# A third tile's rows in early memory, the first tile in halves, and edge scores one row group a step

## The chip, the cores and the metric

The kernel runs on one core of one Trainium2 chip. The metric is the device time of one execution in microseconds (us), as the median of three runs. The core's engines are named as in the profile: PE is TensorE (PEld its weight loads), DVE is VectorE, ACT is ScalarE, POOL is GpSimd, SP is SyncE, which here only issues DMAs. Each engine works through its own list of instructions in order and waits on semaphores.

## What is computed

One graph layer over 1250 nodes of 1024 features, in float32. Cut to what matters (dst also feeds the choice of edges for each window of nodes):

```python
edge_index = jnp.stack([src, dst])            # 41250 edges, sorted by dst
xn = _layernorm(x, axis=-1)
x = x + gnn(xn, edge_index, W, b)             # relu(A_norm @ (xn @ W) + b)
      + linear_attention(xn, Wq, Wk, Wv, Wo)  # phi = elu + 1, 16 heads, S = phi(K)^T V
x = x + ffn(_layernorm(x, axis=-1))           # two gated, two gelu layers, one out
```

The change touches only the first `_layernorm`, the K/V projection that follows it, and the preparation of the edge lists.

## The kernel before

The 1250 rows are 10 tiles of 128 (the last 98). Weights come as slices of 128x512; each is split into a high part (`weight_hi`, a rounding copy, on ACT here) and a low part (`weight_lo`, the difference, on POOL or DVE), and each product is three matmuls (lines 1383 to 1385 for rows in tiles).

The part around the change is a loop of 40 steps that all engines run in step with each other, `s, t = divmod(step, 10)`: weight slab s (256 columns of K beside 256 of V), row tile t. While slab 0 is worked, the ten tiles are also normalised and transposed, a few steps ahead.

- **SP** issues the loads of x: tiles 0 and 1 at once into the two buffers of `xrow`, then the edges, biases and scales, then tile t as soon as `xn_ready` says that tile t-2 is normalised.
- **DVE** in step n: `transposed_lo(n+1)` (L951), an item of edge work if there is one, then, once PE has finished the unit, `kb` (L1109) and `kmin` (L1110), `ln_stats(n+3)` (L921 to L923), `phik` (L1122), `ksum`, `ln_finish(n+3)` (L939 to L944). Edge work: step 1 `edge_keys`, 2 `edge_constants`, 3 `edge_ranges` with the first of three `edge_score`, 4 the other two, 5 `edge_most` (raises `score_ready`), 8 `edge_bounds` (raises `bounds_ready`).
- **ACT** in step n: `transposed_hi(n+1)` (L695), `ln_apply(n+2)` (L688, raises `xn_ready`), the exponential (L742), the copy of V (L746), `ln_root(n+3)` (L674, a square root).
- **PE** in step n: `transpose_tile(n+1)` (L1365, eight matmuls), the unit's 24 matmuls, then `kv_sum(n-1)` (L1398). Step 0's unit has `transpose_tile(1)` in its middle.
- **POOL** loads ten weight slices, makes the identity for the transposes, some low parts, then constants, among them the zeroing of `st_blk` (L625), reloads, and `partition_all_reduce` (L637) once `score_ready` is raised; behind it stand the low parts of slices 8 and 9, the first of slab 1.

Before the loop, tile 2 takes part in neither the first loads nor the first statistics: it needs the buffer of tile 0, and its statistics stand behind `transposed_lo(0)` and three low parts of weights on DVE, its root and `ln_finish(2)` in step 0. `st_blk` ([128, 8, 128] float32, 4 KB a partition, as much as one tile's rows) holds the block matrix of the attention sums, which is filled only after the 40 steps.

Of the kernel before, what the change touches and what calls it, by code (L numbers as in the profile page):

```python
# [31 lines left out]
P = 128  # L32
# [72 lines left out]
def rows(t):  # L105
    return min(P, N - t * P)
# [50 lines left out]
def build(nc, x, src_cols, dst_cols, dst_rows, wslices, wo, bkv, bq, gb, bo, scales, w3s, out):  # L157
    with ExitStack() as ctx:
# [3 lines left out]
        def sem(name):  # L162
            return ctx.enter_context(nc.semaphore(name))
# [107 lines left out]
        x_in = [sem(f"x_in{i}") for i in range(2)]  # L271
# [155 lines left out]

        def xrows(d, t):
            return d[t * P:t * P + rows(t), :]
# [5 lines left out]
        def _(sp):  # L435
            sp.dma_start(xrow[:, 0, :], xrows(x, 0)).then_inc(x_in[0], 16)
            sp.dma_start(xrow[:, 1, :], xrows(x, 1)).then_inc(x_in[1], 16)
# [7 lines left out]
            for t in range(2, NT):  # L445
                sp.wait_ge(xn_ready, t - 1)
                sp.dma_start(xrow[0:rows(t), t % 2, :], xrows(x, t)).then_inc(x_in[t % 2], 16)
# [143 lines left out]
        def _(pool):  # L591
# [33 lines left out]
            nc.gpsimd.memset(st_blk[:], 0.0).then_inc(consts, 1)  # L625
# [8 lines left out]
            for n in range(KD):  # L634
                reload(n)
            pool.wait_ge(score_ready, 1)
# [34 lines left out]
        def _(act):  # L671
# [5 lines left out]
            def ln_apply(i):  # L677

                t = tile_of(i)
                r = rows(t)  # L680
                act.wait_ge(rstd_ready, i + 1)
                if i >= 2:
                    act.wait_ge(tr_done, 2 * (i - 1))
                if i < NT:
                    to, of = xn[0:r, i % 2, :], xrow[0:r, i % 2, :]
                else:
                    to, of = xn2[0:r, i % 2, :], xr[0:r, (i - NT) % XR_BUFS, :]
                nc.scalar.activation(to, of, ACT.Identity, bias=ln[0:r, i % 2, 5:6],  # L688
                                     scale=ln[0:r, i % 2, 4:5]).then_inc(xn_ready, 1)
# [25 lines left out]
            hi(0)  # L715
            hi(1)
            ln_apply(0)
# [3 lines left out]
            ln_root(1)  # L721
            hi(4)
# [4 lines left out]
            for step in range(40):  # L727
# [3 lines left out]
                if step == 0:  # L731
                    ln_root(2)
# [25 lines left out]
            act.wait_ge(consts, 3)  # L758
# [149 lines left out]
        def _(dve):  # L908
# [7 lines left out]
            def ln_stats(i):  # L916
                t = tile_of(i)
                r = rows(t)
                src = xrow[0:r, i % 2, :] if i < NT else xr[0:r, (i - NT) % XR_BUFS, :]
                for g in range(2):  # L920
                    link(dve.bn_stats(stats[0:r, i % 2, 6 * g:6 * g + 6], src[:, 512 * g:512 * g + 512]))  # L921
# [33 lines left out]
            def edge_keys():  # L955

                dve.wait_ge(edges_in, 48)
                dve.wait_ge(consts, 7)
# [15 lines left out]
            def edge_ranges():  # L974
# [5 lines left out]
                edge_score(0)  # L980

            def edge_scores():
                edge_score(1)
                edge_score(2)
# [97 lines left out]
            dve.wait_ge(x_in[0], 16)  # L1082
# [3 lines left out]
            ln_stats(1)  # L1086
            transposed_lo(0)
            weight_lo(dve, LO_FIRST[0])
            ln_finish(1)
            for n in LO_FIRST[1:]:  # L1090
                weight_lo(dve, n)
            dve.wait_ge(x_in[0], 32)
            ln_stats(2)
            edge_parts = {1: edge_keys, 2: edge_constants, 3: edge_ranges, 4: edge_scores, 5: edge_most, 8: edge_bounds}
            dve_more = None
            for step in range(40):
# [5 lines left out]
                if step == 0:  # L1102
                    ln_finish(2)
                if step in edge_parts:
                    edge_parts[step]()
                u = UNIT["kv", s, t]
# [4 lines left out]
                if step < 7:  # L1111
                    dve.wait_ge(x_in[(step + 3) % 2], 16 * ((step + 3) // 2 + 1))
                    ln_stats(step + 3)
# [235 lines left out]
        def _(pe):  # L1349
# [5 lines left out]
            def transpose_tile(i):  # L1355
# [3 lines left out]
                pe.wait_ge(xn_ready, i + 1)  # L1359
                if i >= 1:  # L1360
                    pe.wait_ge(tr_lo, 2 * i)
                for g in range(2):
                    for j in range(4):
# [306 lines left out]
```

## Time and profile before

| what | value |
|---|---|
| median of 3 runs | 1035.27 us (1034.58 to 1037.59) |
| profiled execution | 1034.41 us, span 1032.5 us |
| PE busy | 994.2 us, 96% of the span |
| DVE busy | 555.1 us, 54% |
| ACT busy | 296.0 us, 29% |
| POOL busy | 142.6 us, 14% |
| chain that ended last | PE 83%, DVE 8%, POOL 3%, issue 3%, ACT 2%, DMA 1% |

The span is measured from the first instruction to the last; the execution's own time has about 1.9 us more around it. The shares of the chain are those of the work that ended last, followed back from the end; PE's share of it, not its busy share, says how much of the time PE itself sets.

### The profile page before, as it was taken

What the parts mean: (1) busy time and instruction counts of PE and PEld (TensorE: products, weight loads), DVE (VectorE), ACT (ScalarE), POOL (GpSimd) and SP (SyncE); (2) the same over time, 40 slices, a digit from 0 to 9 for tenths busy, and PEclk for the clock granted to TensorE, in tenths of its full rate; (3) what the DMA queues carried; (4) which work ended last, traced back from release to release, by engine and by line L of the source; (5) the groups of instructions that cost most, each with busy time, mean ns of one, the idle gap of its engine ahead of it and who ended that gap; (6) DMA issues with size and microseconds to landing.
All of it is one profiled execution on the core that took longest, in us unless ns stands there. A gap on an engine that the chain in (4) does not pass through costs nothing.

```text
span 1032.5 us, 13194 instructions
## 1 busy us (share of the span) xinstructions
PE 994.2 (96%) x4932; PEld 839.0 (81%) x4932; DVE 555.1 (54%) x1033; ACT 296.0 (29%) x566; POOL 142.6 (14%) x192
## 2 busy tenths in 40 slices
PE   4999999999998998999999999999999999999998
PEld 3878887887888987977778688758878899999986
DVE  5886768778754785874111356455555413112354
ACT  5783213213115341341212322122212312135300
POOL 7011001001002023041120000000300303055100
PEclk9999999999999998999999999999999999999999
DMA  7313103013002012121130266444521502010053
GB/s 279 108 53 91 29 18 108 17 32 95 15 28 83 25 45 93 45 91 52 41 104 13 80 210 193 160 166 133 189 77 62 164 1 82 1 41 1 16 188 134
DMA packets 43965, 86.74 MB, mean 84 GB/s; under 512 B 16138, under 2 KB 20598, under 8 KB 43880
## 3 DMA queue, kind: packets, MB, share of 16 engines
q1 hardware_dynamic: 35400, 57.20, 16.7%
q0 software_dynamic: 8480, 28.45, 8.6%
q8 instruction: 48, 0.79, 0.3%
q14 instruction: 37, 0.30, 0.1%
HBM read 61.38 MB, written 23.76 MB: 82 GB/s over the span
## 4 chain that ended last, share of the span: by engine, by line
PE 83%; DVE 8%; POOL 3%; issue 3%; ACT 2%; DMA 1%; DVEq 0%; POOLq 0%; ACTq 0%
PE PS L1383 9%; PE PS L1384 9%; PE PS L1385 9%; PE PS L1489 8%; PE PS L1490 8%; PE PS L1491 8%; PE PS L1547 5%; PE PS L1549 4%; PE PS L1566 3%; PE PS L1567 3%; PE PS L1568 3%; PE PS L1422 3%; POOL ring L425 2%; PE PS L1617 2%; PE PS L1619 2%
## 5 line engine op out<-in xcount | busy, mean ns | idle before, releaser
L1383 PE MATMUL PS<-ring,act_t 128*128 128x512 f32 (+1 forms) x480 | 196.2, 409 | 4.6 <-POOL ring L425 3.8
L1385 PE MATMUL PS<-ring,act_t 128*128 128x512 f32 (+1 forms) x480 | 191.8, 400 | 0.0
L1384 PE MATMUL PS<-ring,act_t 128*128 128x512 f32 (+1 forms) x480 | 191.8, 400 | 0.0
L1489 PE MATMUL PS<-act_t,ring 128*128 128x416 f32 (+1 forms) x432 | 161.0, 373 | 7.8 <-POOL ring L425 5.2
L1490 PE MATMUL PS<-act_t,ring 128*128 128x416 f32 (+1 forms) x432 | 153.4, 355 | 0.0
L1491 PE MATMUL PS<-act_t,ring 128*128 128x416 f32 (+1 forms) x432 | 152.9, 354 | 0.0
L1383 PEld LDWEIGHTS PS<-ring,act_t 128*128 128x128 f32 (+1 forms) x480 | 90.7, 189 | 29.1 <-POOL ring L425 6.7
L1385 PEld LDWEIGHTS PS<-ring,act_t 128*128 128x128 f32 (+1 forms) x480 | 90.3, 188 | 22.7
L1384 PEld LDWEIGHTS PS<-ring,act_t 128*128 128x128 f32 (+1 forms) x480 | 90.4, 188 | 21.2 <-issue 0.5
L1489 PEld LDWEIGHTS PS<-act_t,ring 128*128 128x128 f32 x432 | 82.1, 190 | 14.2 <-POOL ring L425 6.8
L1490 PEld LDWEIGHTS PS<-act_t,ring 128*128 128x128 f32 x432 | 82.2, 190 | 4.3 <-issue 3.6
L1491 PEld LDWEIGHTS PS<-act_t,ring 128*128 128x128 f32 x432 | 82.1, 190 | 0.9
L1182 DVE RECIPROCAL rec<-rec 128x416 f32<-128x416 f32 (+1 forms) x24 | 65.9, 2747 | 0.0
L706 ACT ACTIVATE ctile<-PS 128x160 uint16<-128x160 f32 x80 | 23.4, 301 | 143.6 <-PE PS L1422 142.7
L600 POOL DMA_DIRECT2D stage_x<-in_wslices_dram x48 | 26.0, 547 | 211.7 <-DVE ring L425 207.5
L1040 DVE TENSOR_TENSOR oh_dst<-iota,kcur 128x960 bf16<-128x960 int16 x80 | 52.0, 650 | 0.0
L425 POOL TENSOR_TENSOR ring<-stage,ring 128x512 fp32r<-128x512 f32 x27 | 36.3, 1346 | 108.1 <-ACT ring L712 106.5
L1109 DVE TENSOR_TENSOR kb<-PS,kvb 128x256 f32<-128x256 f32 (+1 forms) x40 | 16.9, 424 | 58.0 <-issue 41.7
L1320 DVE SCALAR_TENSOR_TENSOR hb<-PS,scl,sil 128x416 f32<-128x416 f32 (+1 forms) x12 | 7.8, 651 | 73.1 <-PE PS L1491 73.1
L600 POOL DMA_DIRECT2D stage<-in_wslices_dram x48 | 26.5, 553 | 139.0 <-DVE ring L425 131.5
L1039 DVE TENSOR_TENSOR oh_src<-iota,kcur 128x768 bf16<-128x768 int16 x80 | 44.1, 552 | 0.3
L1422 PE MATMUL PS<-oh_dst,oh_src 128*128 128x160 bf16 x480 | 43.2, 233 | 0.0
(186 smaller groups left out, 1658.8 us busy)
## 6 DMA issues: line engine op xcount, KB each, us to landing
stage<-in_wslices_dram POOLq DMA_DIRECT2D x48, 256.0 KB, 3.2
stage_x<-in_wslices_dram POOLq DMA_DIRECT2D x48, 256.0 KB, 3.2
xr<-x_d SPq DMA_DIRECT2D x18, 512.0 KB, 3.4
phin_d<-phiq SPq DMA_DIRECT2D x8, 625.0 KB, 3.2
xrow<-in_x_dram SPq DMA_DIRECT2D x9, 512.0 KB, 3.7
xh<-in_x_dram SPq DMA_DIRECT2D x18, 256.0 KB
x_d<-xh SPq DMA_DIRECT2D x18, 256.0 KB
x_d<-xr SPq DMA_DIRECT2D x9, 512.0 KB, 2.8
```

The source lines that it names most:

```text
L425: eng.tensor_tensor(ring[:, slot(k), 1, :], stage_buf(n), ring[:, slot(k), 0, :].bitcast(F32), ALU.subtract).then_inc(w_ready, 1)
L600: pool.dma_start(stage_buf(n), wslices[n]).then_inc(stage_in[stage_slot(n)], 16)
L1040: dve.tensor_tensor(oh_dst[:, b], count(WCOLS), pairs(kcur[:, dt % 2, j, 1], WCOLS), ALU.is_equal).then_inc(onehot, 1)
L1182: dve.reciprocal(rec[:, i % 2, 0:n], rec[:, i % 2, 0:n]).then_inc(rec_ready, 1)
L1383: pe.matmul(out_ap, node_rows(0, k, t), ring[:, slot(k0 + k), 0, :], start=(k == 0), stop=False)
L1384: pe.matmul(out_ap, node_rows(1, k, t), ring[:, slot(k0 + k), 0, :], start=False, stop=False)
L1385: ins = pe.matmul(out_ap, node_rows(0, k, t), ring[:, slot(k0 + k), 1, :], start=False, stop=(k == KD - 1))
L1422: ins = pe.matmul(PS[:, b, 0:WCOLS], oh_src[:, o, j // 2, :, j % 2], oh_dst[:, o, j // 2, :, j % 2], start=(j == 0), stop=(j == STATIC_CHU ...
L1489: pe.matmul(out_ap, w[0], x_t[:, 0, k, o:o + n], start=(k == 0), stop=False)
L1490: pe.matmul(out_ap, w[0], x_t[:, 1, k, o:o + n], start=False, stop=False)
L1491: ins = pe.matmul(out_ap, w[1], x_t[:, 0, k, o:o + n], start=False, stop=(k == nk - 1))
L1547: pe.matmul(out_ap, lhs, h_rows(half, 0, st), start=(st == 0), stop=False)
```

## The change

Tile 2's rows are loaded into the memory of `st_blk` right behind tiles 0 and 1, ahead of the edge loads on SP. Tile 3 then takes buffer 0 and tile 4 buffer 1, each one tile earlier than before. Tile 2's statistics and root move ahead of the first transposed tile's low part, and its `ln_finish` follows tile 1's. `st_blk` is zeroed by POOL after tile 2 is normalised. Tile 0 is loaded as two halves of 512 columns on two semaphores and normalised in two halves, which now stands ahead of the copy of weight slice 1 on ACT; the first four transposes wait for the first half only. The three `edge_score` stand in steps 4, 5 and 6 and `edge_most` in step 7.

```diff
+        def x_buf(t):
+            return t if t < 3 else (t - 3) % 2
+        def x_uses(t):
+            return 16 * sum(0 < u <= t and x_buf(u) == x_buf(t) for u in range(NT))
+        def x_tile(t):
+            b = x_buf(t)
+            return xrow[0:rows(t), b, :] if b < 2 else st_blk[0:rows(t)].rearrange("p a b -> p (a b)")
...
-            sp.dma_start(xrow[:, 0, :], xrows(x, 0)).then_inc(x_in[0], 16)
-            sp.dma_start(xrow[:, 1, :], xrows(x, 1)).then_inc(x_in[1], 16)
+            for g in range(2):
+                sp.dma_start(xrow[:, 0, 512 * g:512 * g + 512], x[0:P, 512 * g:512 * g + 512]).then_inc(x_first[g], 16)
+            for t in range(1, 3):
+                sp.dma_start(x_tile(t), xrows(x, t)).then_inc(x_in[t], 16)
...
-            for t in range(2, NT):
-                sp.wait_ge(xn_ready, t - 1)
-                sp.dma_start(xrow[0:rows(t), t % 2, :], xrows(x, t)).then_inc(x_in[t % 2], 16)
+            for t in range(3, NT):
+                sp.wait_ge(xn_ready, t - 1 if t > 4 else t - 2)
+                sp.dma_start(x_tile(t), xrows(x, t)).then_inc(x_in[x_buf(t)], 16)
...
-            nc.gpsimd.memset(st_blk[:], 0.0).then_inc(consts, 1)
...
+            pool.wait_ge(xn_ready, 3)
+            nc.gpsimd.memset(st_blk[:], 0.0).then_inc(consts, 1)
             pool.wait_ge(score_ready, 1)
...
+                if i == 0:
+                    nc.scalar.activation(to[:, 0:512], of[:, 0:512], ACT.Identity, bias=ln[0:r, 0, 5:6],
+                                         scale=ln[0:r, 0, 4:5]).then_inc(xn_first, 1)
+                    to, of = to[:, 512:D], of[:, 512:D]
...
             ln_root(0)
             hi(0)
+            ln_apply(0)
             hi(1)
-            ln_apply(0)
             hi(2)
             hi(3)
             transposed_hi(0)
             ln_root(1)
+            ln_root(2)
...
-                if step == 0:
-                    ln_root(2)
...
                 for g in range(2):
+                    if i == 0:
+                        dve.wait_ge(x_first[g], 16)
                     link(dve.bn_stats(stats[0:r, i % 2, 6 * g:6 * g + 6], src[:, 512 * g:512 * g + 512]))
...
             ln_stats(1)
+            dve.wait_ge(x_in[2], 16)
+            ln_stats(2)
             transposed_lo(0)
             weight_lo(dve, LO_FIRST[0])
             ln_finish(1)
+            ln_finish(2)
             for n in LO_FIRST[1:]:
                 weight_lo(dve, n)
-            dve.wait_ge(x_in[0], 32)
-            ln_stats(2)
-            edge_parts = {1: edge_keys, 2: edge_constants, 3: edge_ranges, 4: edge_scores, 5: edge_most, 8: edge_bounds}
+            edge_parts = {1: edge_keys, 2: edge_constants, 3: edge_ranges, 7: edge_most, 8: edge_bounds}
...
-                if step == 0:
-                    ln_finish(2)
                 if step in edge_parts:
                     edge_parts[step]()
+                if 4 <= step < 4 + ROWS_T:
+                    edge_score(step - 4)
...
-                pe.wait_ge(xn_ready, i + 1)
-                if i >= 1:
+                if i:
+                    pe.wait_ge(xn_ready, i + 1)
                     pe.wait_ge(tr_lo, 2 * i)
                 for g in range(2):
+                    if i == 0:
+                        pe.wait_ge(xn_ready if g else xn_first, 1)
```

## Rows read from the trace of the kernel before

**Rows 1.** The waits of TensorE, 0 to 110 us: total, times, longest
```profile
PE PS L1365 <- ACT xn L688: 14.8, 4, 9.6
```

**Rows 2.** Busy time by stretch: PE, PEld, DVE, ACT, POOL, PEclk, DMA share, GB/s
```profile
20.60:23.90 3.30, 0.01 (x1) 0.01 (x1) 3.12 (x10) 1.28 (x2) 3.17 (x6) 0.81 0.84 269
23.90:29.40 5.50, 5.50 (x17) 4.73 (x18) 3.64 (x13) 5.15 (x8) 0.00 (x0) 0.50 0.88 311
```

**Rows 3.** The chain that ended last, 60 to 96 us: start, duration, what
```profile
63.17 1.08 PE PS L1365 x8
...
70.28 0.87 PE PS L1365 x8
...
77.17 0.68 PE PS L1365 x8
...
83.44 0.44 PE PS L1398 x4
...
89.45 0.44 PE PS L1398 x4
```

**Rows 4.** Timeline of the start, 9 to 13 us
```profile
9.23 0.15 DVE L923 TENSOR_SCALAR ln<-mv 128x1 f32<-128x1 f32 x1
...
10.31 0.63 ACT L712 ACTIVATE ring<-stage 128x512 fp32r<-128x512 f32 x1 [0.32 <-DMA stage<-in_wslices_dram]
10.85 0.58 ACT L695 ACTIVATE act_t<-PS 128x512 fp32r<-128x512 f32 x1
11.46 1.45 DVE L951 TENSOR_TENSOR act_t<-PS,act_t 128x512 fp32r<-128x512 f32 x2 [2.08 <-ACT act_t L695]
...
12.21 0.80 PE L1383 MATMUL PS<-ring,act_t 128*128 128x512 f32 x1 [0.65 <-DVE act_t L951]
```

**Rows 5.** Timeline from 18 to 26 us
```profile
18.46 1.41 DVE L921 BATCH_NORM_STATS2 stats<-xrow 128x6 f32<-128x512 f32 x2
...
20.16 0.40 PE L1385 MATMUL PS<-ring,act_t 128*128 128x512 f32 x1
...
22.60 1.24 ACT L688 ACTIVATE xn<-xrow,ln 128x1024 f32<-128x1024 f32 x1 [2.06 <-DVE ln L944]
...
23.89 1.97 PE L1365 MATMUL PS<-ident,xn 128*128 128x128 f32 x8 [3.34 <-ACT xn L688]
```

**Rows 6.** Timeline of DVE, 29 to 58 us
```profile
29.71 0.33 DVE L959 TENSOR_SCALAR e_hi<-e_src 128x336 int32<-128x336 int32 x1
...
30.81 0.51 DVE L963 SCALAR_TENSOR_TENSOR keys<-e_dst,e_hi 128x336 f32<-128x336 int32 x1
...
38.89 0.12 DVE L967 MEMSET key_off<- 128x80 int16 x1
...
40.43 0.42 DVE L1109 TENSOR_TENSOR kb<-PS,kvb 128x256 f32<-128x256 f32 x1
...
46.13 0.19 DVE L976 MEMSET smax<- 128x160 f32 x1
...
47.73 0.28 DVE L990 TENSOR_SCALAR score<-thr,d_rng 108x80 f32<-108x80 f32 x1
...
49.05 0.42 DVE L1109 TENSOR_TENSOR kb<-PS,kvb 128x256 f32<-128x256 f32 x1
...
57.31 0.42 DVE L1109 TENSOR_TENSOR kb<-PS,kvb 128x256 f32<-128x256 f32 x1
```

**Rows 7.** The DMA queues, 5 to 10 us: packets, MB, share of 16 engines
```profile
q0 software_dynamic: 403, 1.34, 68.3%
q1 hardware_dynamic: 441, 0.58, 32.6%
```

**Rows 8.** Timeline of POOL, 60 to 80 us
```profile
63.72 0.87 POOL L637 PARTITION_ALL_REDUCE sall<-smax  x1 [39.95 <-DVE smax L997]
71.43 1.28 POOL L425 TENSOR_TENSOR ring<-stage_x,ring 128x512 fp32r<-128x512 f32 x1 [6.84 <-issue]
...
73.79 1.31 POOL L425 TENSOR_TENSOR ring<-stage_x,ring 128x512 fp32r<-128x512 f32 x1
```

More of the change, by code:

```diff
@@ L270, in build @@
         small_in = sem("small_in")
-        x_in = [sem(f"x_in{i}") for i in range(2)]
+        x_first = [sem(f"x_first{i}") for i in range(2)]
+        x_in = [sem(f"x_in{i}") for i in range(3)]
+        xn_first = sem("xn_first")
         kvb_in = [sem(f"kvb_in{i}") for i in range(2)]
@@ L684, in ln_apply @@
                 if i < NT:
-                    to, of = xn[0:r, i % 2, :], xrow[0:r, i % 2, :]
+                    to, of = xn[0:r, i % 2, :], x_tile(i)
                 else:
                     to, of = xn2[0:r, i % 2, :], xr[0:r, (i - NT) % XR_BUFS, :]
+                if i == 0:
+                    nc.scalar.activation(to[:, 0:512], of[:, 0:512], ACT.Identity, bias=ln[0:r, 0, 5:6],
+                                         scale=ln[0:r, 0, 4:5]).then_inc(xn_first, 1)
+                    to, of = to[:, 512:D], of[:, 512:D]
                 nc.scalar.activation(to, of, ACT.Identity, bias=ln[0:r, i % 2, 5:6],
@@ L757, in _ @@
             nc.scalar.activation(deg[:, 1, :], deg[:, 0, :], ACT.Sqrt).then_inc(root_deg, 1)
-            act.wait_ge(consts, 3)
+            act.wait_ge(consts, 7)
             s_ps = PS[:, 3:5, :].rearrange("p a (b c) -> p (a b) c", c=P)
@@ L918, in ln_stats @@
                 r = rows(t)
-                src = xrow[0:r, i % 2, :] if i < NT else xr[0:r, (i - NT) % XR_BUFS, :]
+                src = x_tile(i) if i < NT else xr[0:r, (i - NT) % XR_BUFS, :]
                 for g in range(2):
+                    if i == 0:
+                        dve.wait_ge(x_first[g], 16)
                     link(dve.bn_stats(stats[0:r, i % 2, 6 * g:6 * g + 6], src[:, 512 * g:512 * g + 512]))
@@ L957, in edge_keys @@
                 dve.wait_ge(edges_in, 48)
-                dve.wait_ge(consts, 7)
+                dve.wait_ge(consts, 6)
                 link(dve.tensor_scalar(e_hi[:], e_src[:], 7, None, ALU.logical_shift_right))
@@ L979, in edge_ranges @@
                 link(dve.tensor_scalar(d_rng[a, 0, :], d_rng[a, 0, :], 1.0 - WIN, None, ALU.add))
[L980 to L984, printed above, removed]
             def edge_score(t):
@@ L1079, in count_tile @@
                 link(dve.tensor_reduce(cmx[:, dt:dt + 1], csum[:, dt % 2, :], AX.X, ALU.max))
-            dve.wait_ge(x_in[0], 16)
             ln_stats(0)
@@ L1111, in _ @@
                 if step < 7:
-                    dve.wait_ge(x_in[(step + 3) % 2], 16 * ((step + 3) // 2 + 1))
+                    dve.wait_ge(x_in[x_buf(step + 3)], x_uses(step + 3))
                     ln_stats(step + 3)
```

## The prediction, made before the changed kernel ran

> **What bounds the kernel now.** I read the page's busy shares first (the table above): PE is busy 96% of the span, so a change can only pay where PE waits or where it is slowed. The view of waits then says where that is: in the first 110 us PE waits 14.8 us for normalised rows, in four waits, the longest 9.6 us, which is the start itself [rows 1]. The windows and the timeline place the next: PE's last matmul of step 0 starts at 20.16 and lasts 0.40, so it is done at 20.56, and the transposes of tile 2 start at 23.89 after 3.34 us of idleness [rows 5]. That leaves 14.8 - 9.6 - 3.3 = 1.9 us in two later waits. The stretch behind the long wait shows a second price: from 23.9 to 29.4 us PE is busy all the time at a granted clock of 0.50, the lower level of 1.2 GHz [rows 2]. Those 5.6 us up to about 29.5 hold what takes half at 2.4 GHz, so 2.8 us are lost to the clock.
>
> Tile 2 is late because of DVE's order: its statistics start at 18.46, its rows are applied at 22.60 [rows 5], while buffer, transposed tile 0 and three low parts stand ahead.
>
> **The pace without waits.** The chain of work gives it: transposes start at 70.28 and again at 77.17, so a step of PE is 6.89 us [rows 3]. The step with tile 9's transposes is 83.88 - 77.17 = 6.71, the step without any 89.89 - 83.88 = 6.01 (each the end of the key sum) [rows 3].
>
> **Part 1: tile 2 early.** Its statistics now come before transposed tile 0, and `ln_finish(2)` behind `ln_finish(1)`. ACT applies tile 2 right after the copies of tile 1, at about 19 us, in 1.24 us [rows 5], done before PE asks at 20.56. The 3.34 us go. PE also doesn't idle, so I take the clock to stay up. From 23.89 to 77.17 the kernel before needs 53.28 us for seven steps [rows 3, 5]; at 6.89 they are 48.23. That is 5.05 us: 2.8 of clock, 1.9 of the two waits, and 0.35 of slow starts around these. Sum so far: -8.4.
>
> **Part 2: edge scores spread.** What stops the 5.05 from coming whole is DVE. From one `kb` to the next, 49.05 to 57.31, is 8.26 us with two scores [rows 6]. One score is 49.05 - 47.73 = 1.32 [rows 6], so a bare cycle is 5.62. The other items are 31.32 - 29.71 = 1.61 (keys), 40.43 - 38.89 = 1.54 (constants), 47.73 - 46.13 = 1.60 (ranges) [rows 6]. In the new order the cycles of steps 1 to 6 are 7.23, 7.16, 7.22 and three of 6.94, in all 42.43 against PE's 41.34: DVE falls 1.1 us behind. Its cover: from `kb` at 57.31 to the transposes that it feeds at 63.17 are 5.86 us [rows 3, 6], and PE asks 6.89 after it starts step 1: 1.03 us of slack at the beginning. So slack and shortfall cancel, and each step's handover is within 0.1 us of due. I charge +0.3, bounds 0 and 1.0 (the whole shortfall). In the old order with tile 2 early it would be worse: step 3 with 8.54 and step 4 with 8.26.
>
> **Part 3: more bytes ahead of the weights.** PE's first real matmul starts at 12.21, released by the low part (11.46), released by the high part (10.85), which stands on ACT behind the copy of weight slice 3 (10.31 to 10.94), which itself waited for its DMA [rows 4]. That load decides the start. From 5 to 10 us the two queues move 403 packets (1.34 MB, weights) and 441 packets (0.58 MB, edges, 1.3 KB each) [rows 7]: turns by packet, not by byte. Tile 2's 128 rows of 4 KB now stand in the place of the first 130 edge packets (0.17 MB), so 0.35 MB more go by at 1.92 MB in 5 us: 0.9 us. Bounds: 0, if the load isn't what is late, and 1.4, if all 0.52 MB go first. I take +0.9.
>
> The Trainium skill ("DMA: Bandwidth & Descriptors", section "Queues, rings and completion order") says that each DMA engine goes round between the queues with work at packet granularity; near-equal packet counts agree, and this rule speaks against the change. By a split of bytes in equal halves instead, the weights would lose nothing and the sum would be 0.9 us lower.
>
> Tile 2 itself should land at about 8.6 us (1.05 MB of tiles 0 and 1 are through at about 5, then 0.52 MB at half of 0.38 MB per us, and some 0.8 to land); DVE is done with tile 1's statistics at 9.38 [rows 4]. 1.76 us of statistics end near 11.1, and the low part isn't due before 11.46. Covered; without the cover it would be at most those 1.76 us.
>
> **Part 4: the first tile in halves.** Worth nothing here. It makes the transposes start some 1.5 us sooner, but what follows them is behind slice 3's copy, as above. Moving the copy of slice 1 behind it costs nothing either: it ends at 9.5 at the latest, and slice 3's copy can't start before 10.31. Two loads of 2 KB rows instead of one: the small packets of [rows 7] move 0.58 MB in a 32.6% share, 1.78 MB per full share, against 1.96 for the large ones, so 10% of 0.26 + 0.26 MB, 0.1 us, inside Part 3's bounds.
>
> **Part 5: the tail of slab 0.** `score_ready` comes two steps later, and POOL has the first low parts of slab 1 behind it. The score's end at 63.51 to slice 8's low part at 71.43 is 7.9 us (0.87 of it the reduction, 6.84 an idle "issue") [rows 8], and slice 9's ends at 75.10, 11.6 behind [rows 8]. New clock: PE starts step 1 at 20.56 + 0.9 = 21.5, step 8 at 21.5 + 48.23 + 0.3 = 70.0, step 9 at 76.7 and slab 1 at 82.7. `edge_most` ends at about 70.2, slice 8 is ready at 79.4, slice 9 at 81.8; due at 82.7 and 83.4. DVE's six low parts follow from 81.8 at 0.76 each, due at 0.70 each from 84.1: covered by 1.3 us or more. DVE gets to `kb` of step 9 at 86.4, 4 us late, and its sums are ready about 88.5, when PE wants them at 88.3 to 88.8. Here the cover is some 0.3 us. I charge +0.3, bounds 0 and 1.5. `edge_bounds` in step 8 needs only the reduction, ready near 71.3. Zeroing `st_blk` (0.96 us) moves to POOL's 40 us wait for the score and is free; SP's waits come no later than before. Nothing behind step 12 changes, and PE sets the pace there, so what is gained stays.
>
> **Sum.** -3.34 - 5.05 + 0.3 + 0.9 + 0.3 = -6.9 us. The profiled execution would go from 1034.41 to 1027.5. It lies 0.86 below the median of the runs shown; on the median it is 1035.27 - 6.9 = 1028.4.
>
> **Rivals.**
> - *Earlier transposes bring the clock up earlier.* PE begins some 1.5 to 1.9 us sooner with transposes. If these count, the first unit has up to 1.9 us less at the lower clock, worth half of it, 0.9, and with Parts 3 and 5 near zero the time is about 1026.5. Against: in step 0 the transposes come before a gap, and PE will idle longer behind them. The Trainium skill ("TensorE: Matmul & The Clock Gate", section "Part 4: PE-mode transpose") says that transposes don't count as busy in the same way; no row here separates it. 0.12.
> - *A new wait takes part of it.* DVE or POOL is late at step 5 to 10: the full shortfall of 1.0, 1.4 for the loads, 1.5 in the tail, -8.4 + 3.9 = -4.5, and if the clock comes up later in the first unit as well, 1 to 1.7 more: 1030.8 to 1032. For it: margins of 0.1 and 0.3. 0.17.
> - *No change that can be measured.* Idle moves rather than goes: a gap of some 3 us opens again between steps 1 and 8 and takes the clock down for 5.5 us, as after 20.56: 3.3 + 2.8 back of 6.9, about 1034.5. 0.07.
> - *Slower: tile 2's load is late.* `ln_stats(2)` stands ahead of transposed tile 0 on DVE, and PE's start is behind that. It decides from the landing time: every us after 9.7 costs one, and from about 17 on all 6.9 are gone; landing at 19, behind all ten weight slices, gives 1037 to 1039. Against: queue order puts it right behind tile 1. 0.04.
> - The forecast, 1027 to 1030.5: 0.60.
>
> **Range and chances.** The range holds the forecast and reaches to the first two rivals: 1026.2 to 1032.0. About 0.3%, 3.1 us, is what a measurement of this kernel can tell from no change. Faster 0.88, the same 0.08, slower 0.04.
>
> **What the profile after would show.** Tile 2's transposes directly behind step 0's last matmul, with no idle time and a granted clock of 1.00 through 20 to 30 us; the first real matmul at about 13.1, behind a copy of slice 3 that starts at about 11.2; steps of 6.9 to 7.0 from 21.5 on; step 8 at about 70; the reduction on POOL near 70 and no wait of PE for weights at 83. If the first matmul starts after 14, or PE waits for `ln_apply` in steps 3 to 7 by over 0.5 us each, Parts 3 or 2 are wrong. If the clock falls anyway, Part 1 is.

## The result, and the profile after

The changed kernel takes 1029.95 us (median of 6 runs, 1029.33 to 1031.73) against 1035.15 us for the kernel before on the same chip. The ratio is 0.9944, with a 95% interval of 0.9923 to 0.9964: 5.2 us less by the medians, 3.7 to 8.0 by the interval. The forecast was 1028.4 with a range of 1026.2 to 1032.0, and "faster". Run a second time beside the experiments, the same code gave 1029.94 against 1033.63, a ratio of 0.9956 (0.9942 to 0.9970), so 3.7 us (3.1 to 6.0). The gain is real. The 6.9 us forecast lie inside the first interval and outside the second.

The waits of PE in the first 110 us (what waits, for whom: total, times, longest) answer to [rows 1]. They were 14.8 us for normalised rows in four waits.

```profile
PE PS L1384 <- ACT xn L706: 9.6, 1, 9.6
PE PS L1402 <- DVE act_t L973: 2.7, 1, 2.7
PE PS L1384 <- ACT xn L709: 0.4, 2, 0.2
PE PS L1417 <- DVE phik L1139: 0.2, 1, 0.2
```

The 3.3 us wait before tile 2 is gone, and of the two in steps 5 and 6 (1.9 us) 0.2 are left in step 5; as little is new in step 8. What is new stands in the second line: 2.7 us between the first transposes and the first real matmul, 0.65 before. The windows (PE, PEld, DVE, ACT, POOL busy, granted clock, DMA share, GB/s) show the same from the other side, and answer to [rows 2]:

```profile
12.20:14.20 2.00, 0.01 (x1) 0.01 (x1) 1.90 (x6) 2.00 (x7) 1.22 (x1) 1.00 1.03 384
...
22.80:29.70 6.90, 6.90 (x37) 5.73 (x36) 6.27 (x17) 5.46 (x9) 2.86 (x5) 1.00 0.78 261
```

Where the clock stood at 0.50 for 5.5 us, it is now 1.00, and PE doesn't pause. The step that held the slow stretch, from tile 2's transposes to tile 3's, took 9.52 us (23.89 to 33.41) and takes 6.95 (22.85 to 29.80): 2.6 us. But from 12.2 to 14.2 PE does nothing, while the DMA engines are full. The timeline of the start answers to [rows 4]:

```profile
8.10 0.63 ACT L733 ACTIVATE ring<-stage 128x512 fp32r<-128x512 f32 x1 [2.29 <-DMA stage<-in_wslices_dram]
...
9.36 1.42 DVE L943 BATCH_NORM_STATS2 stats<-xrow 128x6 f32<-128x512 f32 x2 [2.36 <-DMA xrow<-in_x_dram]
...
11.68 1.42 DVE L943 BATCH_NORM_STATS2 stats<-st_blk 128x6 f32<-128x512 f32 x2 [0.47 <-DMA st_blk<-in_x_dram]
11.90 0.63 ACT L733 ACTIVATE ring<-stage 128x512 fp32r<-128x512 f32 x1 [0.55 <-DMA stage<-in_wslices_dram]
12.44 1.07 ACT L716 ACTIVATE act_t<-PS 128x512 fp32r<-128x512 f32 x2
...
13.45 1.28 DVE L973 TENSOR_TENSOR act_t<-PS,act_t 128x512 fp32r<-128x512 f32 x2
...
14.19 0.79 PE L1402 MATMUL PS<-ring,act_t 128*128 128x512 f32 x1 [2.67 <-DVE act_t L973]
```

The copy of slice 3 starts at 11.90 instead of 10.31, after 0.55 us of waiting for its DMA. Even slice 0's (8.10) waited 2.29 us for its DMA. Tile 1's rows are in only at 9.36 and tile 2's at 11.68, so tile 2's statistics, which stand ahead on DVE, hold transposed tile 0's low part until 13.45, although its high part was there at 13.0. Real work starts at 14.19: 1.98 us later. The first unit, from there to its last matmul (22.61), then takes 8.42 us, where the kernel before took 7.95 (12.21 to 20.16); experiments 4 and 8 return to this.

Steps 0 to 3, from the same timeline and DVE's own, answer to [rows 5, 6]:

```profile
20.80 1.25 ACT L709 ACTIVATE xn<-st_blk,ln 128x1024 f32<-128x1024 f32 x1
...
22.61 0.40 PE L1404 MATMUL PS<-ring,act_t 128*128 128x512 f32 x1
...
22.85 1.03 PE L1384 MATMUL PS<-ident,xn 128*128 128x128 f32 x8
```

```profile
23.05 0.42 DVE L1126 TENSOR_TENSOR kb<-PS,kvb 128x256 f32<-128x256 f32 x1 [1.29 <-PE PS L1404]
23.51 0.77 DVE L1127 TENSOR_SCALAR kmin<-kb 128x256 f32<-128x256 f32 x1
...
30.65 0.42 DVE L1126 TENSOR_TENSOR kb<-PS,kvb 128x256 f32<-128x256 f32 x1
...
37.86 0.42 DVE L1126 TENSOR_TENSOR kb<-PS,kvb 128x256 f32<-128x256 f32 x1
...
45.16 0.42 DVE L1126 TENSOR_TENSOR kb<-PS,kvb 128x256 f32<-128x256 f32 x1
...
52.10 0.43 DVE L1126 TENSOR_TENSOR kb<-PS,kvb 128x256 f32<-128x256 f32 x1
```

Tile 2 is normalised at 22.05, before PE asks for it, and its transposes follow the last matmul without a gap. The cycles from `kb` to `kb` are 7.60, 7.21, 7.30 and 6.94 us. The kernel's next transposes and sums on PE (61 to 96 us) answer to [rows 3]:

```profile
72.23 0.89 PE L1384 MATMUL PS<-ident,xn 98*128 98x98 f32 x8 [0.15 <-ACT xn L709]
...
78.55 0.61 PE L1417 MATMUL PS<-phik,vt 128*128 128x128 f32 x4
...
84.55 0.61 PE L1417 MATMUL PS<-phik,vt 128*128 128x128 f32 x4
...
90.96 0.71 PE L1417 MATMUL PS<-phik,vt 98*128 98x128 f32 x4 [0.23 <-DVE phik L1139]
91.51 0.62 PE L1426 MATMUL PS<-ksum,kvb 128*128 128x128 f32 x4
```

and the tail on POOL and on DVE to [rows 8]:

```profile
72.78 0.87 POOL L654 PARTITION_ALL_REDUCE sall<-smax  x1 [47.12 <-DVE smax L1014]
80.89 1.28 POOL L427 TENSOR_TENSOR ring<-stage_x,ring 128x512 fp32r<-128x512 f32 x1 [7.24 <-ACT ring L733]
```

```profile
84.66 3.08 DVE L427 TENSOR_TENSOR ring<-stage,ring 128x512 fp32r<-128x512 f32 x4 [3.78 <-POOL ring L427]
```

Slab 0's last sums (L1426, L1407 before) start at 91.51 instead of 95.75. So 4.24 us are gained by then, and the span is 4.0 us shorter, 1028.5 for 1032.5. What the change touches ends there.

**How to compare these runs.** From those sums to the end of the span, 936.8 us are left before and 937.0 after. In the fourteen profiles of this study that remainder lies between 935.2 and 941.8, with no relation to what the edit was: the second profile of the changed kernel has 940.2. In that profile, and in the one with 941.8, the granted clock is 0.98 from 600 to 700 us, where it is 1.00 in the first profile of the changed kernel and in the kernel before. One total therefore can't settle a term of 1 us. The experiments are read by places on PE instead: the first real matmul, the start of tile 2's transposes (T2), and from there the start of tile 9's (T9) and of slab 0's last sums (S).

| kernel | first matmul | unit | T2 | T2 to T9 | T9 to S | S | MB from 2 to 5 us |
|---|---|---|---|---|---|---|---|
| before | 12.21 | 7.95 | 23.89 | 53.11 | 18.75 | 95.75 | 1.00 |
| changed | 14.19 | 8.42 | 22.85 | 49.38 | 19.28 | 91.51 | 0.74 |
| changed, again | 12.59 | 7.75 | 20.58 | 49.16 | 19.15 | 88.89 | 1.02 |
| halves undone | 12.02 | 8.37 | 20.62 | 49.14 | 19.36 | 89.12 | 0.96 |
| only the load undone | 12.08 | 9.10 | 21.42 | 48.59 | 19.33 | 89.34 | 0.94 |
| loads of 64 rows | 14.51 | 8.02 | 22.77 | 49.04 | 18.79 | 90.60 | 0.72 |
| scores as they were | 13.42 | 8.47 | 22.13 | 51.55 | 18.74 | 92.42 | 0.77 |
| tile 2 early alone | 12.68 | 8.39 | 21.31 | 51.93 | 18.73 | 91.97 | 0.98 |
| scores spread alone | 12.08 | 9.08 | 23.85 | 49.85 | 18.81 | 92.51 | 0.99 |
| halves alone | 12.19 | 7.96 | 23.72 | 53.24 | 18.73 | 95.69 | 0.94 |
| low parts first | 12.89 | 8.86 | 21.98 | 49.80 | 18.78 | 90.56 | 0.94 |
| weights held back | 15.94 | 8.57 | 24.74 | 49.32 | 19.32 | 93.38 | 0.92 |
| edge work early | 12.13 | 8.01 | 20.37 | 48.41 | 18.74 | 87.52 | 0.96 |
| start reordered too | 11.23 | 9.87 | 21.82 | 48.27 | 18.74 | 88.83 | 1.02 |

All starts are raw ones of the timeline. "Unit" is the time from the first real matmul to the last of step 0's 24. The last column adds the two queues of the DMA view. Each row is one profile, and the second profile of the changed kernel reaches S 2.62 us before the first, so a difference of a microsecond between two rows isn't by itself the work of the edit. The unit alone differs by 1.35 us (7.75 to 9.10) between kernels in which PE waits for nothing inside it.

### The profile page after: what moved, and what is told of

It reads as the page before. It is cut to its first block, busy times and chain, and to the rows that moved or that the text cites. A ratio compares the mean times of both kernels' runs of the same rounds, so it can differ in the third digit from the quotient of the medians.

```text
span 1028.5 us, 13197 instructions
## 1 busy us (share of the span) xinstructions
PE 992.2 (96%) x4932; PEld 837.0 (81%) x4932; DVE 555.2 (54%) x1033; ACT 296.0 (29%) x567; POOL 142.7 (14%) x192
## 4 chain that ended last, share of the span: by engine, by line
PE 80%; DVE 10%; POOL 3%; issue 3%; ACT 2%; DMA 2%; SPq 0%; DVEq 0%; POOLq 0%; ACTq 0%
PE PS L1508 8%; PE PS L1509 8%; PE PS L1510 8%; PE PS L1402 8%; PE PS L1403 8%; PE PS L1404 8%; PE PS L1566 5%; PE PS L1568 4%; PE PS L1585 3%; PE PS L1586 3%; PE PS L1587 3%; PE PS L1441 3%; POOL ring L427 3%; PE PS L1636 2%; PE PS L1638 2%
## 5 line engine op out<-in xcount | busy, mean ns | idle before, releaser
L1404 PEld LDWEIGHTS PS<-ring,act_t 128*128 128x128 f32 (+1 forms) x480 | 90.2, 188 | 22.8
L1508 PEld LDWEIGHTS PS<-act_t,ring 128*128 128x128 f32 x432 | 82.0, 190 | 14.2 <-POOL ring L427 6.7
L427 POOL TENSOR_TENSOR ring<-stage,ring 128x512 fp32r<-128x512 f32 x27 | 36.4, 1347 | 109.3 <-ACT ring L733 107.8
```

The costliest lines, as they stand in the source:

```text
L427: eng.tensor_tensor(ring[:, slot(k), 1, :], stage_buf(n), ring[:, slot(k), 0, :].bitcast(F32), ALU.subtract).then_inc(w_ready, 1)
L1404: ins = pe.matmul(out_ap, node_rows(0, k, t), ring[:, slot(k0 + k), 1, :], start=False, stop=(k == KD - 1))
L1508: pe.matmul(out_ap, w[0], x_t[:, 0, k, o:o + n], start=(k == 0), stop=False)
```

## The experiments

My theory after the result: the three parts work as forecast, and the missing 1.7 us or more are at the start (the loads), in DVE's first cycle and in the tail of slab 0. The rivals: the late start is from tile 2's bytes alone; the steps have slack; the tail stands on something else. Each expectation is as it stood before its run.

**1. Halves undone.** The changed kernel with tile 0 whole:

```diff
-            for g in range(2):
-                sp.dma_start(xrow[:, 0, 512 * g:512 * g + 512], x[0:P, 512 * g:512 * g + 512]).then_inc(x_first[g], 16)
-            for t in range(1, 3):
+            for t in range(3):
                 sp.dma_start(x_tile(t), xrows(x, t)).then_inc(x_in[t], 16)
...
-                if i == 0:
-                    nc.scalar.activation(to[:, 0:512], of[:, 0:512], ACT.Identity, bias=ln[0:r, 0, 5:6],
-                                         scale=ln[0:r, 0, 4:5]).then_inc(xn_first, 1)
-                    to, of = to[:, 512:D], of[:, 512:D]
```

> The changed kernel with tile 0 loaded by one DMA and normalised by one operation; everything else as changed. Question: why the first real matmul starts at 14.19 us instead of 12.21. Theory A (tile 2's bytes stand ahead of the weights; the halves cost nothing): first real matmul at 13.8 to 14.3, copy of slice 3 at 11.7 to 12.0, time within 0.5 us of the changed kernel (1030). Theory B (the two half loads slow the first 5 us, in which 0.74 MB arrived instead of 1.00): first real matmul at 12.9 to 13.3, copy of slice 3 at about 11.2, time about 1029.

Measured: 1027.57 us against 1033.80, ratio 0.9936 (0.9916 to 0.9955). The first real matmul comes at 12.02. That is even earlier than theory B had it, and theory A falls: with tile 2's 0.52 MB ahead of the weights the start isn't late at all. The copy of slice 3 ends at 10.75 (copies of slices 1 to 3: 9.00, 1.75 us for three, with no wait for a DMA).

**2. Only the load undone.** One DMA for tile 0, still normalised in halves.

> The changed kernel with tile 0 loaded by one DMA but still normalised in two halves. Theory (only the load costs): first real matmul at 12.0 to 12.5, as with tile 0 whole in both (12.02); the halved normalising itself is worth at most 0.3 us, since slice 3's copy on ScalarE stands ahead of the transposed tile. Rival (the second, longer operation, 2 x 0.80 for 1.24 us, is the cost): 12.4 to 13.

Measured: 1027.63 us against 1033.78, ratio 0.9946 (0.9926 to 0.9966), first matmul at 12.08. Whether the normalising is halved makes no difference to the start (12.02 and 12.08); the load is what does. T2 is 0.8 us later than in experiment 1 all the same, since the unit takes 9.10 us for 8.37. The DMA view from 2 to 5 us (packets, MB, share of the 16 engines), first of this kernel and then of the changed one:

```profile
q1 hardware_dynamic: 246, 0.94, 84.5%
q0 software_dynamic: 1, 0.00, 0.4%
```

```profile
q1 hardware_dynamic: 292, 0.58, 56.1%
q0 software_dynamic: 47, 0.16, 41.7%
```

These are the two kernels' rows in that order. With one load, SP's queue has the engines nearly to itself and brings 0.94 MB. With two short loads, the weights' queue comes in early, with 47 packets instead of 1, and these 47 take 41.7% of 48 engine-microseconds, 0.43 us each, where a packet of theirs takes 0.14 us in [rows 7] (68.3% of 80 for 403). SP's own packets bring 0.58 MB. The second profile of the same kernel is milder: 75 packets of the weights' queue at 0.15 us each, 0.77 MB on SP's, 1.02 together, as much as in the kernel before.

**3. Rows or DMAs?** Tile 0's two loads cut by rows, so that they have 4 KB rows as before:

```diff
-                sp.dma_start(xrow[:, 0, 512 * g:512 * g + 512], x[0:P, 512 * g:512 * g + 512]).then_inc(x_first[g], 16)
+                sp.dma_start(xrow[64 * g:64 * g + 64, 0, :], x[64 * g:64 * g + 64, :]).then_inc(x_first[g], 16)
```

> The changed kernel with tile 0's two loads cut the other way: 64 rows of 4 KB each instead of 128 rows of 2 KB; the same bytes, the same number of DMAs, half the rows to describe. The statistics wait for both. Theory (SP's queue brings about 90 to 100 rows per us, however long they are): about 0.95 MB from 2 to 5 us, first real matmul at 12.0 to 12.7. Rival (one more DMA is what costs): 0.55 to 0.6 MB and first matmul at 13.4 to 14.2 as in the changed kernel.

Measured: 1029.38 us against 1033.78, ratio 0.9955 (0.9939 to 0.9972), first matmul at 14.51. The theory of rows falls:

```profile
q1 hardware_dynamic: 127, 0.45, 61.9%
q0 software_dynamic: 81, 0.27, 37.7%
```

The rows are 4 KB and there are fewer of them, and SP's queue is slower still. The start is lost at another place here: the statistics wait for both loads, and tile 0's begin at 6.85 instead of 4.34. Two short first loads cost, however they are cut; whether by their length or because there is one more of them, these runs don't separate.

**4. Halves alone.** The kernel before with tile 0 in halves and nothing else.

> The kernel before with tile 0 in halves alone (two loads of 2 KB rows, two operations of normalising, slice 1's copy behind them). Theory (the two half loads slow the first 5 us, whatever else is early): 0.55 to 0.60 MB on SP's queue from 2 to 5 us instead of 0.94 to 0.98, first real matmul 13.0 to 13.8 instead of 12.2, time 0.8 to 1.6 us over the kernel before. Rival (only together with tile 2's load): first matmul 12.2, time unchanged.

Measured: 1032.59 us against 1033.78, ratio 0.9991 (0.9979 to 1.0004): no difference. The rival holds: the first matmul is at 12.19. SP's queue is slowed here too (0.71 MB for 0.98), but there is 0.5 MB less to bring before the weights, and slice 3's copy stays at 10.29. PE's timeline of this run bears on the rival of the clock:

```profile
7.74 1.97 PE L1375 MATMUL PS<-ident,xn 128*128 128x128 f32 x8 [7.74 <-POOL ident L608]
12.19 0.80 PE L1393 MATMUL PS<-ring,act_t 128*128 128x512 f32 x1 [2.48 <-DVE act_t L960]
...
15.35 0.61 PE L1394 MATMUL PS<-ring,act_t 128*128 128x512 f32 x1
15.77 0.42 PE L1395 MATMUL PS<-ring,act_t 128*128 128x512 f32 x1
16.03 0.39 PE L1393 MATMUL PS<-ring,act_t 128*128 128x512 f32 x1
```

The transposes begin at 7.74 instead of 9.62, the real matmuls at 12.19 instead of 12.21, and the matmuls change from 0.43 us apart to 0.23 at 15.8 to 16.0, where the kernel before did it too. Matmuls 0.43 us apart are what the kernel before has at a granted clock of 0.50 (26.08 to 29.07), so I read them as the 1.2 GHz level. The windows view doesn't show that level at the start; in the changed kernel it has

```profile
14.10:19.00 4.90, 4.81 (x12) 3.80 (x13) 3.68 (x14) 3.28 (x6) 2.00 (x2) 1.00 1.04 319
```

over matmuls that are 0.43 us apart up to 18.6. In this profile the earlier transposes brought no earlier clock. One pair of profiles doesn't settle it, as experiment 8 shows.

**5. Weights held back.** To see whether the two queues hinder each other, POOL waits with its first weight load until tile 0 is in:

```diff
+            pool.wait_ge(x_first[1], 16)
             for n in range(STAGE_A):
                 load(n)
```

> The changed kernel with GpSimd's first weight loads held back until both halves of tile 0 have landed (about 3.7 us instead of 1.2). Theory (the short first loads cost because the weight packets of the other queue start among them and both then move slowly): SP's queue brings 0.9 MB or more from 2 to 5 us as with one load, tile 2 lands by 8.6, and the first real matmul comes at 12.3 to 13.2 although the weights were asked for 2.4 us later. Rival (it is SP's own queue that is slow behind short loads): still 0.6 MB, first real matmul at 14.5 or later.

Measured: 1032.48 us against 1033.63, ratio 0.9985 (0.9969 to 1.0001); first matmul at 15.94. Half of the theory holds: alone, SP's queue brings 0.92 MB in spite of the halves. The time expected doesn't: POOL issues the first weight load at 4.26 instead of 1.24, the first weight copy starts at 11.04 instead of 8.10, and those 3 us cost more than they save.

```profile
q1 hardware_dynamic: 376, 0.92, 96.2%
```

**6. Scores as they were.** The changed kernel with one score in step 3, two in step 4, `edge_most` in step 5.

```diff
-            edge_parts = {1: edge_keys, 2: edge_constants, 3: edge_ranges, 7: edge_most, 8: edge_bounds}
+            edge_parts = {1: edge_keys, 2: edge_constants, 3: edge_ranges, 5: edge_most, 8: edge_bounds}
...
-                if 4 <= step < 4 + ROWS_T:
-                    edge_score(step - 4)
+                for k in {3: (0,), 4: (1, 2)}.get(step, ()):
+                    edge_score(k)
```

> The changed kernel with the edge scores where they were (step 3 one, step 4 two, edge_most in step 5). Theory of the prediction (DVE sets the pace between steps 1 and 8, 5.62 us plus the item of edge work): steps 3 and 4 have cycles of about 8.6 and 8.3 us on DVE, PE waits for normalised rows some 1.4 + 1.4 us in two places, and the transposes of tile 9 start about 1.5 us later than 72.23; time 1031 to 1032. Against it slab 1's first weights come 9 us sooner on GpSimd, which gives back up to 0.5 us in the tail. Rival (DVE's order has slack, the scores are hidden anyway): tile 9's transposes at 72.2, time as the changed kernel or 0.5 us less.

Measured: 1029.46 us against 1033.80, ratio 0.9953 (0.9940 to 0.9966), so not the expected 1031 to 1032, and by the totals no slower than the changed kernel. PE waits where it was expected to:

```profile
51.59 1.08 PE L1384 MATMUL PS<-ident,xn 128*128 128x128 f32 x8 [1.47 <-ACT xn L709]
...
59.85 1.09 PE L1384 MATMUL PS<-ident,xn 128*128 128x128 f32 x8 [1.16 <-ACT xn L709]
```

DVE's cycles are 8.63 and 8.25 us, and T2 to T9 is 51.55 instead of 49.38: 2.17 us. The tail gives 0.54 back (18.74 for 19.28), so between T2 and S the spreading is worth 1.6 us net. The rival, slack on DVE, is out. The totals don't show the 1.6: this profile starts 0.8 us earlier than the first of the changed kernel (13.42 for 14.19) and reaches S 0.9 us later.

**7. Tile 2 early alone, and 8. scores spread alone.** Each on the kernel before.

> The kernel before with tile 2 early alone (no halves, edge scores where they were, slice 1's copy ahead of tile 0's rows). Theory: nearly all of the gain is here. First real matmul at 13.1 by theory B (14.2 by theory A), no idle time before tile 2's transposes, DVE cycles of 8.6 and 8.3 in steps 3 and 4; time 1030.5 to 1032, so 3.5 to 4.5 us under the kernel before. Rival (the early tile only moves the wait): PE idle 2 us or more before tile 3's or 4's transposes and time above 1033.

> The kernel before with the edge scores spread over steps 4, 5 and 6 alone. Theory: it takes the two waits of PE (0.66 and 1.17 us) in steps 5 and 6, about 1.5 to 2 us together with what stands around them, and slab 1's weights come later with 0.0 to 0.5 us lost in the tail; first real matmul stays at 12.2, the idle time of 3.3 us at 20.6 stays; time 1033 to 1034. Rival (those waits come from being late after tile 2, not from the scores): time unchanged.

Measured: tile 2 alone 1030.19 us against 1033.80, ratio 0.9967 (0.9951 to 0.9982), S at 91.97, 3.78 us earlier; the clock stays up behind step 0 and PE waits 2.6 us in steps 5 and 6, where the kernel before waited 1.8:

```profile
51.11 1.08 PE L1375 MATMUL PS<-ident,xn 128*128 128x128 f32 x8 [1.52 <-ACT xn L703]
...
59.35 1.08 PE L1375 MATMUL PS<-ident,xn 128*128 128x128 f32 x8 [1.09 <-ACT xn L703]
```

Scores alone 1030.69 us, ratio 0.9969 (0.9956 to 0.9982), S at 92.51, 3.24 us earlier. That is more than the expected 1.5 to 2. T2 to T9 falls by 3.26 us, of which 2.2 are the waits and slow starts; the other microsecond is the clock, which came back at about 28.4 here and at 29.5 before, after an idle time of 2.3 us instead of 3.3. That idle time is shorter because step 0 ended later, and that isn't the edit's doing: this kernel's code differs from the one before only from step 3 on, yet its first unit takes 9.08 us for 7.95, with matmuls still 0.43 us apart up to tile 1's transposes:

```profile
16.94 0.63 PE L1382 MATMUL PS<-ring,act_t 128*128 128x512 f32 x1
17.36 1.41 PE L1362 MATMUL PS<-ident,xn 128*128 128x128 f32 x8
```

In the kernel before they were 0.23 us apart from 15.8 on. The unit is 1.13 us longer, which at half speed is some 2.3 us more at the low level. That comes from one execution to the next, and the extra microsecond is luck. The two gains add to 7.0; experiment 1, which has both changes and one load, has 6.6 at S (89.12 for 95.75). An overlap of more than 0.4 us isn't shown.

**9. Low parts first.** POOL makes the low parts of slices 8 and 9 before it waits for the scores:

```diff
             nc.gpsimd.memset(st_blk[:], 0.0).then_inc(consts, 1)
+            for n in range(8, 10):
+                weights(n)
             pool.wait_ge(score_ready, 1)
...
-            for n in range(8, 42):
+            for n in range(10, 42):
```

> The changed kernel with the low parts of slices 8 and 9 on GpSimd ahead of its wait for the scores. Theory (the tail loses 0.5 us because DVE stands 3.8 us behind those low parts): from tile 9's transposes to the end of slab 0's sums 18.75 instead of 19.28 us, no wait of PE for the sums, DVE's low parts from about 81 instead of 84.7; time 0.5 us less than the changed kernel. Rival: DVE's 3.8 us stood on nothing that PE needs, and the 0.5 us are from elsewhere: 19.28 stays.

Measured: 1028.01 us against 1033.78, ratio 0.9939 (0.9921 to 0.9957). T9 to S is 18.78, and DVE reaches `kb` of step 9 at 84.92 instead of 89.25: the theory holds for the tail. But the low parts now meet DVE in step 0, and its first cycle grows to 8.01 us. In DVE's timeline `phik`, 0.42 us elsewhere, takes 1.25:

```profile
24.66 1.25 DVE L1141 SCALAR_TENSOR_TENSOR phik<-kb,kexp 128x256 f32<-128x256 f32 x1
```

and in POOL's timeline a low part runs beside it, from 24.28:

```profile
24.28 1.34 POOL L427 TENSOR_TENSOR ring<-stage_x,ring 128x512 fp32r<-128x512 f32 x1
```

So it gives 0.5 us in one place and takes 0.4 in another.

**10. Edge work early.** One load for tile 0, and the edge work put where DVE can carry it and where POOL is done in time:

```diff
-            edge_parts = {1: edge_keys, 2: edge_constants, 3: edge_ranges, 7: edge_most, 8: edge_bounds}
+            edge_parts = {1: edge_keys, 2: edge_ranges, 6: edge_most, 7: edge_constants, 8: edge_bounds}
...
-                if 4 <= step < 4 + ROWS_T:
-                    edge_score(step - 4)
+                if 3 <= step < 3 + ROWS_T:
+                    edge_score(step - 3)
```

> The changed kernel with tile 0 loaded by one DMA, and the edge work as keys 1, ranges 2, scores 3 to 5, most 6, constants 7. Theory (DVE's cycles of 7.2, 7.2 and 7.3 us set the steps, and the low parts of slices 8 and 9 behind the scores cost the tail): steps 1 to 8 of PE at 6.89 to 6.95 from step 4 on, tile 9's transposes 48.3 to 48.5 us after tile 2's (48.6 to 49.4 in the kernels with the changed order), 18.75 us from there to the end of slab 0's sums instead of 19.3; span 0.5 to 1.2 us under the same kernel with the changed edge order (1025.2). Rival (the steps are PE's already): no difference.

Measured: 1027.02 us against 1033.63, ratio 0.9935 (0.9917 to 0.9952). T2 to T9 is 48.41 and T9 to S 18.74, both as expected; S comes at 87.52, the earliest of all. The span, 1023.0, is 2.2 us under experiment 2's 1025.2, where 0.5 to 1.2 were expected; 1.1 of it is the first unit (8.01 us for 9.10), which the edit doesn't touch. On the same chip the changed kernel, run again, took 1029.94:

> The changed kernel itself, for a comparison on the same chip as the two kernels with one load. Theory (short loads cost 0.9 to 2 us at the start, differently from run to run): first real matmul between 12.9 and 14.3, time 1 to 2 us over the kernel with one load and edge work early, and 5 us under the kernel before. Rival (the late start of the first profile was chance): first matmul at 12.0 to 12.5.

Measured there: ratio 0.9956 (0.9942 to 0.9970), first matmul at 12.59, between the two ranges. The start is late by 0.4 us in this profile and was by 2.0 in the first one. The kernel with the edge work early beats both in the medians, the changed one by 2.9 us and the one before by 6.6. Its interval overlaps the changed kernel's, so only the gain against the kernel before is settled.

**11. Start reordered.** Besides, tile 0's high parts ahead of the copies of slices 2 and 3, and its low part ahead of tile 2's statistics (tile 2's root on ACT moves behind tile 1's rows with them, not shown):

```diff
             hi(1)
+            transposed_hi(0, (0,))
             hi(2)
+            transposed_hi(0, (1,))
             hi(3)
-            transposed_hi(0)
...
-            dve.wait_ge(x_in[2], 16)
-            ln_stats(2)
             transposed_lo(0)
             weight_lo(dve, LO_FIRST[0])
             ln_finish(1)
+            dve.wait_ge(x_in[2], 16)
+            ln_stats(2)
             ln_finish(2)
```

> The kernel with tile 0 loaded by one DMA and the edge work early, and besides: tile 2's statistics behind the low part of tile 0, slice 1, 5 and 7's parts in the old places, and the two high parts of tile 0 ahead of the copies of slices 2 and 3. Theory (the start waits for slice 3's copy and for tile 2's statistics, both ahead of what PE needs): first real matmul at 10.9 to 11.4 instead of 12.05, and the span less by 0.5 to 1.0 us. Rival (the shift is eaten, because weights for the first unit or tile 2's rows then come late): PE waits for slices or for tile 2 and the span is unchanged.

Measured: 1027.18 us against 1033.63, ratio 0.9938 (0.9920 to 0.9956). The first matmul comes at 11.23 and T2 nevertheless at 21.82. PE's waits in the first 30 us show the rival:

```profile
PE PS L1400 <- DVE ring L427: 0.7, 1, 0.7
PE PS L1400 <- DVE act_t L970: 0.6, 1, 0.6
PE PS L1400 <- POOL ring L427: 0.5, 1, 0.5
PE PS L1382 <- DVE act_t L970: 0.3, 1, 0.3
```

The 0.6 is the wait before the first real matmul; the others come behind it. The 0.9 us won at the start are lost again, and 1.5 more: from tile 1's transposes to tile 2's are 5.95 us (15.87 to 21.82) instead of experiment 10's 3.65 (16.72 to 20.37). Of these 2.3 us 1.2 are waits for the low parts of the first unit's own slices (L427), which DVE and POOL now make too late, 0.3 the wait for transposed tile 1, and the rest is what each stop and restart costs besides.

## Why the prediction was right, and where it was not

The sign, the range and the main mechanism were right; the price of the start was not. The sum had 6.9 us; the profile has 4.24 at slab 0's last sums, the second profile of the same code 6.86, the medians 5.2 and 3.7. The terms of the two profiles, in us, from the starts in the table above (the idle time from the start of the unit's last matmul to T2, 3.73 before):

| term | forecast | first profile | second profile |
|---|---|---|---|
| start of real work | +0.9 | +1.98 | +0.38 |
| length of the first unit | none | +0.47 | -0.20 |
| idle time before tile 2 | -3.34 | -3.49 | -3.49 |
| T2 to T9 | -4.75 | -3.73 | -3.95 |
| tail | +0.3 | +0.53 | +0.40 |
| sum | -6.9 | -4.24 | -6.86 |

The second sum is as good as the forecast, but not its terms: a cheap start and a short first unit there make up for what T2 to T9 lacks, and that is luck. By its own steps:

- **Part 1, the idle time.** Right. The 3.34 us are gone in every kernel with tile 2 early, and the clock, 0.50 there before, is 1.00 from 22.8 to 29.7. The 5.05 took tile 9's start from the chain (77.17) and tile 2's from the timeline (23.89); by the timeline alone (77.00) it is 53.11 - 48.23 = 4.88. The clock's part of it was 2.6 (9.52 us for 6.95 in that step), not 2.8. What Part 2 takes back goes off it.
- **Part 2, DVE's balance.** The mechanism was right, the size too small: forecast +0.3, bound 1.0; measured 49.38 against 48.23, +1.15, and +0.93 in the second profile. The cycles were computed as 7.16 and 7.22 and came as 7.21 and 7.30. The first was computed as 7.23 and was 7.60: `kmin` takes 0.77 us there instead of 0.29. With one load for tile 0 `kmin` took 0.29 in experiment 2, and T2 to T9 was 48.59, +0.36; in experiment 1 it took 0.86, and T2 to T9 was +0.91:

```profile
21.28 0.86 DVE L1120 TENSOR_SCALAR kmin<-kb 128x256 f32<-128x256 f32 x1
```

POOL issues its reloads beside it in each of these profiles, so these alone aren't the cause, and what makes `kmin` long stays open. With the loads of 64 rows it took 0.29 and T2 to T9 was +0.81; there, as in both profiles of the changed kernel, `phik` of step 6 starts 2.81 us after `kb` instead of 2.44, behind 0.29 us that the profile puts down to issue. The term has no room for either.
- **Part 3, bytes ahead of the weights.** The step that failed, and its own sign for it came: the first real matmul is at 14.19, after the 14 that it named. It charged +0.9 to tile 2's place in the queue. With whole loads the start is at 12.02 and 12.08 although tile 2 is early (and at 12.68 with the old order on ACT), so that price is 0 to 0.5: in experiments 1 and 2 the copies of slices 1 to 3 run without a wait for a DMA, and it isn't slice 3's load that decides the start. Tile 2 was to land at about 8.6 us; with one load it lands 6.9 us after its issue at 1.64, at 8.5, as worked out. In the changed kernel it takes 9.5 us from 2.12 on and lands at 11.6, outside the cover that I gave it: 0.4 us of the late start is its statistics holding DVE.
- **Part 4, the halves.** "Worth nothing" was right of the normalising (experiments 1, 2 and 4). The 0.1 us for the two loads was wrong: together with tile 2's load, the first matmul is at 12.59, 12.89, 13.42 and 14.19 in four profiles, 0.5 to 2.2 us behind experiments 1, 2 and 10. It was computed from the share of small packets later on, when both queues are full, and said nothing of what happens when the first load is short. The start follows the bytes moved from 2 to 5 us: at 0.94 and 1.02 MB it is 12.9 and 12.6, at 0.77, 0.74 and 0.72 it is 13.4, 14.2 and 14.5. That is not all of it, since whole loads with 0.94 to 0.98 MB start at 12.0 to 12.7. The charge of 0.9 for the start was near the middle of these by luck: the right sum for a wrong cause.
- **Part 5, the tail.** Right in kind, +0.53 (and +0.40) for the +0.3 forecast. `phik` of step 9 is 0.2 us late for PE, as the margin of 0.3 had it at risk. Whether it costs at all depends on when POOL starts slice 8's low part, behind the reduction: 8.1 and 8.2 us after T9 (loads of 64 rows, scores spread alone) it costs less than 0.1, and at 8.5 to 8.7 in both profiles of the changed kernel and in experiments 1, 2 and 5 it costs 0.4 to 0.6. Experiments 9 and 10, which have T9 to S at 18.78 and 18.74, show the place.
- **Rivals.** Earlier clock by earlier transposes: not seen in experiment 4. The Trainium skill ("TensorE: Matmul & The Clock Gate", section "Part 4: PE-mode transpose") says that transposes don't count as busy in the same way, and that profile is in line with it: transposes from 7.74 instead of 9.62, the same rise at 15.8 to 16.0. It doesn't prove it, since the rise moved by some 2.3 us between two kernels with the same code up to there (experiment 8). A new wait that takes part of it: its waits came in part, from the loads mainly, while the time (1029.95) stayed in the forecast's band of 1027 to 1030.5. A clock that comes up later in the first unit, which that rival priced at 1 to 1.7, came as 0.5 in the first profile and as 0.9 to 1.2 in experiments 2, 8 and 9. The other two did not come.

What stays open is why two short first loads let the other queue's packets in and slow SP's queue, why their cost differs from run to run by over a microsecond, and what sets the moment of the clock's rise in the first unit. The experiments show that it is neither the length of the rows nor the halved normalising, and that SP's queue keeps its pace when the weights stay away; they don't show what happens inside the DMA engines.

## What to carry to other kernels

When an engine waits once for a late input and a clock drop follows, the input's own chain (buffer, order on the engine that prepares it) is worth more than its idle time: 3.3 us of idleness stood for another 2.6 at half clock. Moving one tile's preparation forward gave 3.8 us of these by itself, since the next engine's shortage then showed (2.6 us of waits instead of 1.8) and the start came 0.5 us later. Then balance the engine behind it, item by item and cycle by cycle, against the pace of the engine that sets the time, and leave it more than 0.1 us of room. Cut the first load of a kernel only if something waits for its first half: here nothing did, and the cut cost nothing alone and 0.5 to 2 us at the start together with the third load. Look at a second profile before a microsecond at one place is put down to an edit.

## What the runs showed of the hardware that was not expected

- Two short first loads on SP's queue (128 rows of 2 KB, or 64 of 4 KB) bring 0.45 to 0.77 MB on that queue from 2 to 5 us in six profiles, one whole load 0.94 to 1.01 MB in seven. The other queue has 47 to 81 packets there behind short loads and at most 7 behind a whole one. With the other queue held back, SP's brings 0.92 MB in spite of the short loads.
- `phik` on DVE (128x256, 0.42 us) takes 0.52 to 1.25 us once in the first 100 us of each of five profiles, each time with a low part (`TENSOR_TENSOR`) on POOL that began 0.4 to 1.1 us before it: 1.25, 1.19 (experiment 4, at 72.27) and 1.02 (experiment 11, at 71.56) where it began last. Beside POOL's zeroing of `st_blk` it stays at 0.42.
- `kmin` on DVE (128x256 from SBUF to SBUF) takes 0.29 us, and in step 0 0.35 to 1.07 in ten of the fourteen profiles. POOL issues loads beside it in all fourteen.
- The first unit's matmuls are 0.43 us apart at first and 0.23 later, and by when that changes the unit takes 7.75 to 9.10 us without a wait inside it. The windows view has a granted clock of 1.00 there all the same (four profiles looked at).
- A load on the software queue asked for at 1.24 us brings its first packets at 4.8 to 5 us behind whole loads, and at 3.1 to 3.6 behind short ones.
- After the reduction on POOL the next low part starts 7.6 to 8.4 us after the reduction's start in thirteen profiles, of which the reduction is 0.9.
